# Six-stage transformer kernel: where and by which engines the last feed-forward's weights are rounded

## The chip, the cores and the metric

One core of one Trainium2 chip. The metric is device time in microseconds (us) from launch to end, median of several runs. "The profile" is one execution recorded by the hardware; its span runs from the first to the last instruction.

## What is computed

Two decoder layers on `x` of 2 x 512 tokens, width 512, each step followed by a residual add and a layer norm: causal attention with rotary embedding, cross attention with normalised queries and keys, a four-expert feed-forward; then causal attention, masked grouped cross attention, and an 8-bit feed-forward. Each attention has 16 heads of 128. Of the last step (the changed one):

```python
def _reorder_quantize_x(x, idx):
    scale = jnp.max(jnp.abs(x)) / GLOBAL_DIV
    xr = (x / scale)[:, idx]
    scale_x = jnp.max(jnp.abs(xr), axis=1, keepdims=True) / FP8_MAX
    return (_fp8(xr / scale_x), scale_x, scale)

def _qlinear(qx, scale_x, scale, W, idx, out_idx=None):
    Wr = W[:, idx]
    w_scale = jnp.max(jnp.abs(Wr), axis=1, keepdims=True) / FP8_MAX
    qw = _fp8(Wr / w_scale)
    y = qx * scale_x @ (qw * w_scale).T * scale
    ...
```

`w_gate` and `w_up` are 1408 x 512, `w_down` is 512 x 1408. Their rounding depends on no activation, so it can be done at any earlier time.

## The kernel before

**Stages.** The program runs `self0`, `cross0`, `ffn0`, `self1`, `cross1`, `ffn1` in this order. TensorE (PE) does every f32 product as three bf16 products of high and low parts; ScalarE (ACT) writes high parts, VectorE (DVE) low parts. An attention goes over 32 units (head and batch) of four query tiles. Probabilities leave as `ph` and `pl` and are turned by DMA transposes that SyncE's queue (SP) issues one after another (`transposed`). Each engine runs its own list in written order, tied to the others by semaphores.

**The end of an attention.** After unit 31 PE projects heads 0 to 7 with Wo for token tiles 0 to 3 (96 matmuls), weighs the last unit, projects heads 0 to 7 for tiles 6, 7 and then 4, 5 (96 more; tiles 4, 5 wait for `heads_out(31)` on VectorE), and then waits until all of Wo is split (`w_split` at 2H). After that come eight rounds of 24 matmuls, heads 8 to 15 of one tile, each followed by the turning of the normalised tile two before (`turn_x`). Wo for heads 8 to 15 comes head by head: `wo(h)` on SP waits for the split of head h-2 (two buffers of `raw_q`), and `split_wo(h)` on GpSimd (POOL) makes the two parts. The residual add and statistics of a tile are on VectorE (`residual`, `normalise`), the inverse deviation on GpSimd (`inv_std`), which between tiles also splits the next stage's first weights (`start_layer`).

**Rounding the last weights.** There are 26 items (`ITEMS`): 22 of 128 x 512 ("gu", gathered by GpSimd with `indirect_dma_start`, `gather`) and four of 128 x 1408 ("d", loaded by SP, `load_down`). Each goes through `quantise` (VectorE: largest value, scale, inverse), `scaled_weights` (ScalarE), `magnify` (three instructions on VectorE), `round_rows` (one subtraction on GpSimd) and `keep` (SP writes it back to HBM). Items 0 to 7 (`EARLY`) come behind the last unit of `self0`, 8 to 11 (`LATER`) behind `heads_out(31)`, 12 to 14 inside its layer norm. Items 15 to 18, the wide ones, come behind the last unit of `self1`, ahead of `heads_out(31)`; 19 to 22 behind it; 23 to 25 inside its layer norm. SP does `keep` of the early items ahead of `wo(10)`.

**Into cross1 and ffn1.** At the start of `cross1` SP writes the 26 columns of scales to HBM in pieces of 4 bytes (`kept["s"]`) and then loads the mask, spread over 128 partitions. Nothing but the first K products goes without the mask (`any`, `mb`). At the end of `cross1` the rounded weights come back through 19 DMA transposes (`turned`), four behind each `wo(h)` from `wo(10)` on, and then the scales (`sB`). In `ffn1` VectorE multiplies the gate product by its scales (`gate`), ScalarE applies Silu, GpSimd multiplies by the up scales (`times_up`), VectorE multiplies by the up product out of PSUM (`rows`), finds the row scales (`scales`) and rounds (`round_t`); `scales`, `steps` and `round_x` are the same pattern for the activations.

Of the kernel before, what the change touches and what calls it, by code (L numbers as in the profile page):

```python
# [112 lines left out]
def build(nc, a, out, kept):  # L113
    ctx = ExitStack()
    with ctx:
        def sb(name, shape, dt, where=ctx):
# [51 lines left out]
        idx_in, q_a, q_s, q_m, q_ok, s_kept, s_in, wt_in, row_y = (  # L168
            sem(x) for x in ("idx_in", "q_a", "q_s", "q_m", "q_ok", "s_kept", "s_in", "wt_in", "row_y"))
# [3 lines left out]
        fg_mm, fu_mm, g_ok, gs_ok, fs_ok, fy_ok = (sem(x) for x in ("fg_mm", "fu_mm", "g_ok", "gs_ok", "fs_ok", "fy_ok"))  # L173

        idb_ok = sem("idb_ok")
        row_in = [sem(f"row_in{i}") for i in range(4)]
# [60 lines left out]
        for li, L in enumerate(stages):  # L237
# [86 lines left out]
        def slot(k):  # L324

            return k % 4 if k < 15 else (k - 15) % 2 if k < 19 else (k - 19) % 4

        def earlier(k, kind):

            return sum(ITEMS[j][0] == kind and slot(j) == slot(k) for j in range(k))  # L330

        def item_buffers(k):

            m, w = mem[names.index("self0" if k < 15 else "self1")], FI if ITEMS[k][0] == "d" else D
            y, r = (t[:, slot(k) * w:slot(k) * w + w] for t in (m["wy"], m["wr"]))
            s = slot(k) % 2 if k < 15 else slot(k)
            return y, m["wm"][:, s * w:s * w + w], r

        def items_done(k, ring):

            return k - ring + 1 if k < 15 else (k - 1 if k >= 17 else 0) if k < 19 else max(19, k - 3)
# [7 lines left out]
        def _(sp):  # L349
# [23 lines left out]
            for li, L in enumerate(stages):  # L373
# [108 lines left out]
                for k in LATER.get(L.name, ())[:-IN_LN]:  # L482
                    keep(k)
# [6 lines left out]
        def _(pool):  # L490
# [67 lines left out]
            def gather(k):  # L558

                i = ITEMS[k][1]  # L560
                if items_done(k, 4) > 0:
                    pool.wait_ge(q_ok, items_done(k, 4))
                nc.gpsimd.indirect_dma_start(out=item_buffers(k)[0], out_offset=None, in_=a["wgate" if i < IT else "wup"],
                                             in_offset=bass.IndirectOffsetOnAxis(ap=idx[:, i % IT:i % IT + 1].bitcast(mybir.dt.uint32), axis=0)).then_inc(row_in[slot(k)], 16)

            def round_rows(k):

                y, M, q = item_buffers(k)
                pool.wait_ge(q_m, k + 1)
                if k == 19:  # L570
                    pool.wait_ge(q_kept[1], 16 * earlier(18, "gu") + 32)
                if earlier(k, "gu") + earlier(k, "d") and k not in (15, 16):
# [926 lines left out]
```

## Time and profile before

| | |
|---|---|
| median of 3 runs | 2785.51 us (2782.92 to 2787.16) |
| the profiled execution | 2783.92 us, span 2782.1 us |
| mean granted TensorE clock | 0.952 of full speed |
| PE, DVE, ACT, POOL busy | 89%, 67%, 56%, 28% of the span |
| first projection products of heads 8 to 15 | 518.2 us (`self0`), about 1312 (`cross0`), 1921.5 (`self1`), 2573.6 (`cross1`) |

Times in the trace count from the span's start. An idle time in brackets is that of the engine just before the instruction, with the instruction or transfer that ended it. L12 is line 12 of the kernel. Idle time of an engine on which nobody waits costs nothing.

### The profile page before, as it was taken

The page shows a single profiled execution, that of the slowest core. Times are in us where ns is not written, and L with a number is a line of the kernel's source. Part 1 is how long each engine was busy: PE and PEld are TensorE (multiplying, and loading weights), DVE is VectorE, ACT ScalarE, POOL GpSimd, SP SyncE. Part 2 cuts the span into 40 slices and gives each one's busy share as a digit, 9 for nine tenths or more (in the row PEclk, how much of TensorE's full clock was granted, in tenths as well). Part 3 has the DMA queues.
Part 4 walks back from the last instruction along what each step waited for, and adds up shares of the span by engine and source line. Part 5 has one row for each costly group of instructions (what it writes and reads, how often), then busy time and mean ns, then how long its engine had stood idle before and what let it go on. Part 6 is the DMA issues. An engine that isn't in the chain of part 4 may idle for free. (4 is left out here: it accounts for less than half of the span.)

```text
span 2782.1 us, 58623 instructions
## 1 busy us (share of the span) xinstructions
PE 2465.7 (89%) x21584; PEld 1580.1 (57%) x21584; DVE 1854.6 (67%) x3337; ACT 1567.3 (56%) x2692; POOL 778.9 (28%) x705
## 2 busy tenths in 40 slices
PE   6888888879999999999789999995699999997864
PEld 4555555446666666665456666652366666663322
DVE  4667776557777777772565666655488888881687
ACT  4666665148877887882244555530177777771232
POOL 4565666811110011122241222226100011022132
PEclk9999999989999999999899999997799999998886
DMA  3333335425666666665213434343287777786000
GB/s 89 84 70 82 82 71 112 118 44 107 115 117 115 109 109 114 115 126 125 101 59 65 101 79 101 80 111 94 12 149 152 146 145 147 145 164 136 10 0 31
DMA packets 777602, 273.62 MB, mean 98 GB/s; under 512 B 746096, under 2 KB 748912, under 8 KB 775792
## 3 DMA queue, kind: packets, MB, share of 16 engines
q1 hardware_dynamic: 775696, 265.85, 46.1%
q0 software_dynamic: 1760, 5.77, 0.8%
q8 instruction: 98, 1.61, 0.2%
q14 instruction: 48, 0.39, 0.0%
HBM read 84.55 MB, written 6.44 MB: 33 GB/s over the span
## 5 line engine op out<-in xcount | busy, mean ns | idle before, releaser
L860 ACT ACTIVATE ph<-p,ri 128x1024 bf16<-128x1024 f32 (+4 forms) x512 | 437.4, 854 | 473.5 <-DVE ri L1162 396.2
L1172 DVE SCALAR_TENSOR_TENSOR pl<-p,ri,ph 128x1024 bf16<-128x1024 f32 (+4 forms) x512 | 511.7, 1000 | 138.4 <-issue 74.2
L1232 PE MATMUL ps<-wo_hi,v_hi 128*128 128x128 bf16 x2688 | 479.1, 220 | 60.3 <-DMA wo_lo<-pl 59.5
L1234 PE MATMUL ps<-wo_hi,v_lo 128*128 128x128 bf16 x2688 | 478.8, 220 | 0.0
L1233 PE MATMUL ps<-wo_lo,v_hi 128*128 128x128 bf16 x2688 | 478.8, 220 | 0.0
L871 ACT ACTIVATE p<-p,nb 128x1024 f32<-128x1024 f32 (+4 forms) x512 | 435.5, 851 | 46.8 <-DVE nb L1155 36.7
L1232 PEld LDWEIGHTS ps<-wo_hi,v_hi 128*128 128x128 bf16 x2688 | 263.6, 98 | 130.2 <-DMA wo_lo<-pl 80.1
L1232 PE MATMUL ps<-k_hi,q_hi 128*128 128x512 bf16 (+3 forms) x768 | 271.9, 354 | 37.3 <-DVE k_lo L1125 31.0
L1233 PEld LDWEIGHTS ps<-wo_lo,v_hi 128*128 128x128 bf16 x2688 | 263.8, 98 | 38.9
L1234 PE MATMUL ps<-k_hi,q_lo 128*128 128x512 bf16 (+3 forms) x768 | 271.6, 354 | 0.0
L1233 PE MATMUL ps<-k_lo,q_hi 128*128 128x512 bf16 (+3 forms) x768 | 271.5, 354 | 0.0
L1234 PEld LDWEIGHTS ps<-wo_hi,v_lo 128*128 128x128 bf16 x2688 | 264.1, 98 | 0.0
L1232 PE MATMUL ps<-wo_hi,oT_hi 128*128 128x512 bf16 x512 | 199.3, 389 | 54.0 <-POOL wo_lo L517 38.3
L512 POOL TENSOR_SCALAR wkv_hi<-raw_kv 128x1024 bf16<-128x1024 f32 (+1 forms) x56 | 50.6, 903 | 649.5 <-PE ps L1234 457.3
L1232 PE MATMUL ps<-xT_hi,wq_hi 128*128 128x512 bf16 x512 | 198.2, 387 | 24.5 <-DVE k_lo L1117 14.1
L1233 PE MATMUL ps<-wo_lo,oT_hi 128*128 128x512 bf16 x512 | 198.6, 388 | 0.0
L1234 PE MATMUL ps<-wo_hi,oT_lo 128*128 128x512 bf16 x512 | 198.4, 387 | 0.0
L1233 PE MATMUL ps<-xT_lo,wq_hi 128*128 128x512 bf16 x512 | 197.9, 386 | 0.0
L1234 PE MATMUL ps<-xT_hi,wq_lo 128*128 128x512 bf16 x512 | 197.8, 386 | 0.0
L1157 DVE CUSTOM_DVE_ANT_0 p<-ps,rk,nq 128x1024 f32<-128x1024 f32 x128 | 163.2, 1275 | 51.1 <-PE ps L1234 51.0
L634 POOL TENSOR_TENSOR nq<-nq,half_neg 128x4 f32<-128x4 f32 x32 | 32.4, 1012 | 549.1 <-DVE nq L1106 549.1
L1232 PE MATMUL ps<-wkv_hi,xT_hi 128*128 128x128 bf16 x1024 | 179.8, 222 | 0.0
(187 smaller groups left out, 5875.9 us busy)
## 6 DMA issues: line engine op xcount, KB each, us to landing
raw_kv<-in_wkvself SPq DMA_DIRECT2D x32, 512.0 KB
raw_q<-in_wqself SPq DMA_DIRECT2D x32, 256.0 KB
wo_hi<-ph SPq DMA_TRANSPOSE x512, 3.2
wo_lo<-pl SPq DMA_TRANSPOSE x512, 3.1
raw_q<-in_woself SPq DMA_DIRECT2D x32, 256.0 KB
raw_q<-in_wqcross SPq DMA_DIRECT2D x32, 256.0 KB
raw_q<-in_wocross SPq DMA_DIRECT2D x32, 256.0 KB
raw_kv<-in_wkvcross SPq DMA_DIRECT2D x24, 256.0 KB
```

What stands on the lines that cost most here:

```text
L512: nc.gpsimd.tensor_scalar(hi, src, 1.0, 1.0, ALU.mult, ALU.mult).then_inc(w_hi, 1)
L634: nc.gpsimd.tensor_tensor(r, r, half_neg[:, 0:QT], ALU.pow).then_inc(q_norm, 1)
L860: nc.scalar.activation(m["ph"][:, qt % 2, 0:w], m["p"][:, qt % 2, 0:w], ACT.Copy, scale=ri[:, qt % 2:qt % 2 + 1]).then_inc(p_norm, 1)
L871: nc.scalar.activation(prob, prob, ACT.Exp, scale=1.0 if L.rms else -1.0, bias=nb[:, qt % 2:qt % 2 + 1], accum_out=rs[:, qt % 2:qt % 2 + 1 ...
L1157: ins = nc.vector.tensor_tensor_reduce(in1=m["rk"][:, n % 2, :], scale=m["nq"][:, n % 2, qt:qt + 1], op0=ALU.mult, **kw)
L1172: nc.vector.scalar_tensor_tensor(out=m["pl"][:, qt % 2, 0:w], in0=m["p"][:, qt % 2, 0:w], scalar=ri[:, qt % 2:qt % 2 + 1], in1=m["ph"][:, ...
L1232: nc.tensor.matmul(o, l(0), r(0), start=first, stop=False)
L1233: nc.tensor.matmul(o, l(0), r(1), start=False, stop=False)
L1234: return nc.tensor.matmul(o, l(1), r(0), start=False, stop=last)
```

## The change

The wide items move from `self1` to the end of `cross0` and use the memory of `ffn0`'s weights. `self0` takes items 0 to 10 (seven early, four later), `cross0` items 11 to 14, `self1` items 15 to 25 (seven early, four later); none is left inside a layer norm. GpSimd's subtraction goes: ScalarE now writes two scaled copies, and VectorE does one bit operation and two `scalar_tensor_tensor`. The second copy lies in the probabilities' buffer `m["p"]`, so ScalarE first waits for the last `pl`. Gathers have 6 buffers in `self0` and 11 in `self1`, and all are issued in a row behind the last unit. In `cross0` SP waits for the last unit's output, loads two wide items, and puts `keep` and `load_down` of the next ones between `wo(11)`, `wo(12)` and `wo(13)`. In `cross1` the mask is loaded ahead of the 4-byte writes, and `wo(10)` to `wo(15)` go ahead of the 19 transposes. GpSimd starts two pieces of the next stage's weights ahead of the first `inv_std`. In `ffn1` the up product is multiplied by its scales on VectorE (`up`), out of PSUM, and PE's up product of a tile now follows its gate product, two tiles ahead. The core of the diff:

```diff
@@ -310,10 +308,9 @@
-        ITEMS = [("gu", i) for i in range(15)] + [("d", t) for t in range(D // P)] + [("gu", i) for i in range(15, GU)]
-        EARLY = {"self0": range(0, 8), "self1": range(15, 19)}
-        LATER = {"self0": range(8, 15), "self1": range(19, 26)}
-        IN_LN = 3
+        ITEMS = [("gu", i) for i in range(IT)] + [("d", t) for t in range(D // P)] + [("gu", i) for i in range(IT, GU)]
+        EARLY = {"self0": range(0, 7), "self1": range(15, 22)}
+        LATER = {"self0": range(7, 11), "cross0": range(11, 15), "self1": range(22, 26)}
         X_COL, T_COL = GU + D // P, GU + D // P + NT
         HALF_UP = 1.5 * 2.0 ** 14
@@ -354,13 +353,13 @@
             def load_down(k):
                 t = ITEMS[k][1]
-                if items_done(k, 2) > 0:
-                    sp.wait_ge(q_ok, items_done(k, 2))
+                if t >= 2:
+                    sp.wait_ge(q_ok, k - 1)
                 sp.dma_start(item_buffers(k)[0], a["wdown"][t * P:(t + 1) * P, :]).then_inc(wd_in[t % 2], 16)
@@ -408,17 +407,14 @@
-                for k in LATER.get(names[li - 1], ())[-IN_LN:] if li else ():
-                    keep(k)
-                if L.masked:
-                    sp.wait_ge(q_a, len(ITEMS))
-                    sp.dma_start(kept["s"].rearrange("(c p) -> p c", p=P), q_scale[:, 0:X_COL], allow_slow_non_contiguous=True).then_inc(s_kept, 16)
...
                 if L.masked:
                     sp.wait_ge(ln_x, NT * li)
                     sp.dma_start(mem[li]["m8"][:, :, :], a["mask"].partition_broadcast(P)).then_inc(const_in, 16)
+                    sp.wait_ge(q_a, len(ITEMS))
+                    sp.dma_start(kept["s"].rearrange("(c p) -> p c", p=P), q_scale[:, 0:X_COL], allow_slow_non_contiguous=True).then_inc(s_kept, 16)
@@ -455,32 +451,33 @@
-                if L.name == "self1":
-                    load_down(15)
-                    load_down(16)
                 transposed(UNITS - 1, None, QT - 1)
                 wo(8)
                 wo(9)
                 for k in EARLY.get(L.name, ()):
                     keep(k)
-                    if L.name == "self1" and k + 2 < 19:
-                        load_down(k + 2)
+                if L.rms:
+                    sp.wait_ge(o_mm, c["u"] + UNITS)
+                    sp.wait_ge(p_lo, c["s"] + QT * UNITS)
+                    load_down(11)
+                    load_down(12)
+                for h in range(10, H):
+                    wo(h)
+                    if L.rms and h in (11, 12):
+                        keep(h)
+                        load_down(h + 2)
+                for k in LATER.get(L.name, ())[2 if L.rms else 0:]:
+                    keep(k)
                 if L.masked:
                     sp.wait_ge(job_mm, c["job"] + L.before(UNITS + 1))
                     for i in range(4):
-                        sp.wait_ge(q_kept[i], 16 * sum(slot(k) == i for k in range(len(ITEMS))))
+                        sp.wait_ge(q_kept[i], 16 * sum(kept_slot(k) == i for k in range(len(ITEMS))))
+                    for ch in range(2 * XC + IT):
+                        sp.dma_start_transpose(*turned(ch)).then_inc(wt_in, 16)
                     sp.wait_ge(s_kept, 16)
-                for h in range(10, H):
-                    wo(h)
-                    if L.masked:
-                        for ch in range(4 * (h - 10), min(4 * (h - 10) + 4, 2 * XC + IT)):
-                            sp.dma_start_transpose(*turned(ch)).then_inc(wt_in, 16)
-                if L.masked:
...
-                for k in LATER.get(L.name, ())[:-IN_LN]:
-                    keep(k)
@@ -558,22 +555,10 @@
-                if items_done(k, 4) > 0:
-                    pool.wait_ge(q_ok, items_done(k, 4))
+                if k in range(6, 11):
+                    pool.wait_ge(q_ok, k - 5)
...
-            def round_rows(k):
...
-                nc.gpsimd.tensor_tensor(q, y, M, ALU.subtract).then_inc(q_ok, 1)
-                if ITEMS[k][0] == "gu" and k + 4 in range(0, 15 if k < 15 else 26):
-                    gather(k + 4)
@@ -608,17 +593,8 @@
-                    def times_up(t):
-                        pool.wait_ge(fs_ok, t + 1)
-                        nc.gpsimd.tensor_tensor(m["SG"][:, t % 2, :], m["SG"][:, t % 2, :], m["sB"][:, FI:2 * FI], ALU.mult).then_inc(gs_ok, 1)
-
-                    pool.wait_ge(s_in, 16)
-                    times_up(0)
-                    for t in range(NT):
-                        if t + 1 < NT:
-                            times_up(t + 1)
-                        if t:
-                            inv_std(t - 1)
+                    for t in range(NT - 1):
+                        inv_std(t)
                     inv_std(NT - 1)
@@ -675,28 +651,22 @@
-                if L.name == "self0":
+                if L.causal:
                     pool.wait_ge(idx_in, 16)
-                    for k in range(4):
-                        gather(k)
-                for k in EARLY.get(L.name, ()):
-                    round_rows(k)
-                if L.name == "self1":
-                    for k in range(19, 23):
+                    for k in range(0, 11) if L.rope else range(15, 26):
                         gather(k)
                 pool.wait_ge(o_mm, c["u"] + UNITS)
                 for h in range(8, H):
                     split_wo(h)
-                for k in LATER.get(L.name, ())[:-IN_LN]:
-                    round_rows(k)
                 following = stages[li + 1]
                 pieces = range(0) if following is None else range(0 if following.rms else 4, 6)
+                ahead = 2
+                for piece in pieces[:ahead]:
+                    start_layer(li + 1, piece)
                 for t in range(NT):
-                    if t < len(pieces):
-                        start_layer(li + 1, pieces[t])
                     inv_std(t)
-                    if L.name in LATER and t >= NT - IN_LN:
-                        round_rows(LATER[L.name][t - NT])
+                    if t + ahead < len(pieces):
+                        start_layer(li + 1, pieces[t + ahead])
@@ -722,8 +692,11 @@
-                y, n = item_buffers(k)[0], column(k)
+                (y, M, _), n, ring = item_buffers(k), column(k), 1 if ITEMS[k][0] == "d" else 2
                 act.wait_ge(q_a, k + 1)
+                if local(k) >= ring:
+                    act.wait_ge(q_ok, k - ring + 1)
+                nc.scalar.activation(M, y, ACT.Copy, scale=q_up[:, n:n + 1])
                 nc.scalar.activation(y, y, ACT.Copy, scale=q_inv[:, n:n + 1]).then_inc(q_s, 1)
@@ -889,10 +862,12 @@
+                if L.name in EARLY:
+                    act.wait_ge(p_lo, c["s"] + QT * UNITS)
                 for k in EARLY.get(L.name, ()):
                     scaled_weights(k)
                 heads_out(UNITS - 1, None)
-                for k in LATER.get(L.name, ())[:-IN_LN]:
+                for k in LATER.get(L.name, ()):
                     scaled_weights(k)
@@ -901,8 +876,6 @@
                     for t in range(NT):
-                        if L.name in LATER and t >= NT - IN_LN:
-                            scaled_weights(LATER[L.name][t - NT])
                         x_part(li + 1, NT * (li + 1) + t, t, t)
@@ -931,24 +904,22 @@
-            def magnify(k):
-
-                y, M, _ = item_buffers(k)
+                scales(column(k), y).then_inc(q_a, 1)
+
+            def round_item(k):
+
+                y, M, q = item_buffers(k)
                 dve.wait_ge(q_s, k + 1)
-                if items_done(k, 2) > 0:
-                    dve.wait_ge(q_ok, items_done(k, 2))
-                own(nc.vector.tensor_scalar(M.bitcast(I32), y.bitcast(I32), 0x7F800000, None, ALU.bitwise_and))
-                own(nc.vector.tensor_scalar(M, M, 2.0 ** -6, 1.5 * 2.0 ** 20, ALU.max, ALU.mult))
-                nc.vector.tensor_tensor(y, y, M, ALU.add).then_inc(q_m, 1)
+                steps(M)
+                own(nc.vector.scalar_tensor_tensor(out=y, in0=M, scalar=HALF_UP, in1=y, op0=ALU.max, op1=ALU.add))
+                if local(k) >= (1 if ITEMS[k][0] == "d" else 4):
+                    dve.wait_ge(q_kept[kept_slot(k)], kept_count(k))
+                nc.vector.scalar_tensor_tensor(out=q, in0=M, scalar=HALF_UP, in1=y, op0=ALU.max, op1=ALU.subtract, reverse1=True).then_inc(q_ok, 1)
             def quantise_run(ks):
@@ -1048,13 +1019,17 @@
+                    def up(t):
+                        dve.wait_ge(fu_mm, t + 1)
+                        if t >= 2:
+                            dve.wait_ge(qt_ok, t - 1)
+                        nc.vector.tensor_tensor(m["row"][:, t % 2, :], ps[:, 3:6, :].rearrange("p a n -> p (a n)")[:, 0:FI], m["sB"][:, FI:2 * FI], ALU.mult).then_inc(u_ok, 1)
+
                     def rows(t):
                         y = m["row"][:, t % 2, :]
-                        dve.wait_ge(fu_mm, t + 1)
-                        dve.wait_ge(gs_ok, t + 1)
-                        if t >= 2:
-                            dve.wait_ge(qt_ok, t - 1)
-                        nc.vector.scalar_tensor_tensor(out=y, in0=ps[:, 3:6, :].rearrange("p a n -> p (a n)")[:, 0:FI], scalar=q_scale[:, X_COL + t:X_COL + t + 1],
+                        dve.wait_ge(fs_ok, t + 1)
+                        dve.wait_ge(u_ok, t + 1)
+                        nc.vector.scalar_tensor_tensor(out=y, in0=y, scalar=q_scale[:, X_COL + t:X_COL + t + 1],
                                                        in1=m["SG"][:, t % 2, :], op0=ALU.mult, op1=ALU.mult).then_inc(row_y, 1)
                         dve.wait_ge(row_y, t + 1)
@@ -1071,10 +1046,12 @@
+                    up(0)
                     for t in range(NT):
                         rows(t)
                         if t + 1 < NT:
                             gate(t + 1)
+                            up(t + 1)
                         round_t(t)
                         if t:
@@ -1297,7 +1271,7 @@
-                            pe.wait_ge(row_y if part else g_ok, t)
+                            pe.wait_ge(u_ok if part else g_ok, t)
                         for n, (lo, hi) in enumerate(CH):
@@ -1321,13 +1295,13 @@
+                    product(1, 1)
                     turn_qx(c["ln"], m, 6)
                     turn_qx(c["ln"], m, 7)
                     for t in range(NT):
-                        if t + 1 < NT:
-                            product(1, t + 1)
                         if t + 2 < NT:
                             product(0, t + 2)
+                            product(1, t + 2)
                         turn_rows(t)
                         pe.wait_ge(qt_T, t + 1)
                         for i in range(IT):
```

## Rows read from the trace of the kernel before

**Rows 1.** Waits, whole span: total us, times, longest.

```profile
PE ps L1232 <- POOL wo_lo L517: 38.3, 3, 18.2
PE ps L1238 <- DVE xf L1007: 30.2, 12, 5.5
```

**Rows 2.** Timeline of PE, first attention's end: start us, us, [idle before <-what ended it].

```profile
518.17 0.62 PE L1232 MATMUL ps<-wo_hi,oT_hi 128*128 128x512 bf16 x1 [6.53 <-POOL wo_lo L517]
...
581.30 0.61 PE L1232 MATMUL ps<-cT_hi,wkv_hi 128*128 128x512 bf16 x1 [1.42 <-DVE xT_lo L927]
```

**Rows 3.** Timelines of SyncE's queue and GpSimd, first attention's end.

```profile
478.66 19.92 SPq L357 DMA_DIRECT2D kept_gu<-wr  x8
...
501.55 0.34 SPq L426 DMA_DIRECT2D raw_q<-in_woself  x1
...
516.97 1.15 POOL L517 TENSOR_TENSOR wo_lo<-raw_q,wo_hi 128x512 bf16<-128x512 f32 x1
```

**Rows 4.** Groups of instructions, whole span: busy us, mean ns of one | idle before.

```profile
L979 DVE SCALAR_TENSOR_TENSOR xrow<-xM,xrow 128x512 f32<-128x512 f32 x8 | 5.5, 693 | 0.3
L965 DVE TENSOR_REDUCE q_max<-row 128x1 f32<-128x1408 f32 x8 | 13.0, 1620 | 0.3
L972 DVE TENSOR_SCALAR M<-M 128x1408 int32<-128x1408 int32 x8 | 7.2, 894 | 12.3 <-ACT row L779 12.3
L1066 DVE SCALAR_TENSOR_TENSOR row<-M,row 128x1408 f32<-128x1408 f32 x8 | 13.0, 1625 | 0.3
L778 ACT ACTIVATE M<-row,q_up 128x1408 f32<-128x1408 f32 x8 | 11.7, 1468 | 22.7 <-DVE q_up L968 22.7
```

**Rows 5.** Timelines of GpSimd and VectorE, second attention's end.

```profile
1307.89 1.16 POOL L517 TENSOR_TENSOR wo_lo<-raw_q,wo_hi 128x512 bf16<-128x512 f32 x1
...
1317.41 0.69 DVE L999 TENSOR_TENSOR xf<-ps,xf 128x512 f32<-128x512 f32 x1 [24.58 <-PE ps L1234]
...
1355.86 0.69 DVE L999 TENSOR_TENSOR xf<-ps,xf 128x512 f32<-128x512 f32 x1 [2.93 <-PE ps L1234]
...
1360.61 0.69 DVE L927 TENSOR_TENSOR xT_lo<-ps,xT_hi 128x512 bf16<-128x512 f32 x1 [0.18 <-ACT xT_hi L707]
```

**Rows 6.** Windows of 72 matmuls: length; PE, PEld, DVE, ACT, POOL busy; clock; DMA.

```profile
1312.20:1327.74 15.54, 15.54 (x74) 7.17 (x73) 3.59 (x7) 0.00 (x0) 1.80 (x4) 1.00 0.13 52
1921.51:1939.90 18.39, 18.38 (x72) 8.51 (x72) 3.85 (x7) 0.00 (x0) 12.93 (x14) 0.85 0.37 115
```

**Rows 7.** Loads of down-projection rows, issue to landing; their write-backs on SyncE's queue.

```profile
DMA to landing us min/median/max: 4.2/4.4/6.2
...
1865.08 0.34 SPq L357 DMA_DIRECT2D kept_d<-wr  x1
...
1878.36 0.34 SPq L357 DMA_DIRECT2D kept_d<-wr  x1
```

**Rows 8.** Timeline of PE, from the third attention's end into the fourth.

```profile
1895.38 0.62 PE L1232 MATMUL ps<-wo_hi,oT_hi 128*128 128x512 bf16 x1 [15.76 <-DVE oT_lo L1136]
...
1921.51 0.62 PE L1232 MATMUL ps<-wo_hi,oT_hi 128*128 128x512 bf16 x1 [13.51 <-POOL wo_lo L517]
...
1983.27 0.61 PE L1232 MATMUL ps<-cT_hi,wkv_hi 128*128 128x512 bf16 x1 [1.42 <-DVE xT_lo L927]
...
2002.61 0.61 PE L1232 MATMUL ps<-xT_hi,wq_hi 128*128 128x512 bf16 x1 [14.06 <-DVE k_lo L1117]
```

**Rows 9.** DMA issues from 1980 to 2003 us: KB each, us to landing.

```profile
m<-in_mask SPq DMA_DIRECT2D x1, 256.0 KB, 17.5
kept_s<-q_scale SPq DMA_DIRECT2D x1, 13.0 KB, 15.6
```

**Rows 10.** Timeline of PE, fourth attention's end.

```profile
2573.59 0.61 PE L1232 MATMUL ps<-wo_hi,oT_hi 128*128 128x512 bf16 x1 [18.23 <-POOL wo_lo L517]
```

**Rows 11.** Window of one last feed-forward tile; rounding instruction, ns min/median/max.

```profile
2702.73:2719.27 16.54, 11.33 (x46) 5.09 (x46) 14.89 (x15) 5.04 (x5) 5.16 (x4) 0.71 0.00 1
...
L1070 DVE SCALAR_TENSOR_TENSOR Q<-M,row x8: 1625/4454/4467, 2648.8 to 2761.7; 128x1408 bf16<-128x1408 f32 x8
```

More of the change, by code:

```diff
@@ L166, in build @@
         gu_mm, silu_ok, prod_ok, inter_hi, inter_lo = (sem(x) for x in ("gu_mm", "silu_ok", "prod_ok", "inter_hi", "inter_lo"))
-        idx_in, q_a, q_s, q_m, q_ok, s_kept, s_in, wt_in, row_y = (
-            sem(x) for x in ("idx_in", "q_a", "q_s", "q_m", "q_ok", "s_kept", "s_in", "wt_in", "row_y"))
+        idx_in, q_a, q_s, q_ok, s_kept, s_in, wt_in, row_y = (
+            sem(x) for x in ("idx_in", "q_a", "q_s", "q_ok", "s_kept", "s_in", "wt_in", "row_y"))
         wd_in, q_kept = [sem("wd_in0"), sem("wd_in1")], [sem(f"q_kept{i}") for i in range(4)]
@@ L172, in build @@
         t_amax, t_scaled, t_sum, qt_ok, qt_mm, qt_T = (sem(x) for x in ("t_amax", "t_scaled", "t_sum", "qt_ok", "qt_mm", "qt_T"))
-        fg_mm, fu_mm, g_ok, gs_ok, fs_ok, fy_ok = (sem(x) for x in ("fg_mm", "fu_mm", "g_ok", "gs_ok", "fs_ok", "fy_ok"))
+        fg_mm, fu_mm, g_ok, u_ok, fs_ok, fy_ok = (sem(x) for x in ("fg_mm", "fu_mm", "g_ok", "u_ok", "fs_ok", "fy_ok"))
         idb_ok = sem("idb_ok")
-        row_in = [sem(f"row_in{i}") for i in range(4)]
+        row_in = [sem(f"row_in{i}") for i in range(11)]
         by_name = {L.name: L for L in LAYERS}
@@ L322, in column, with local, kept_slot, kept_count @@
             return ITEMS[k][1] + (GU if ITEMS[k][0] == "d" else 0)
[L324 to L330, printed above, removed]
+        def local(k):
+            return k if k < 11 else k - 11 if k < 15 else k - 15
         def item_buffers(k):
[L334 to L341, printed above, removed]
+            j = local(k)
+            if ITEMS[k][0] == "d":
+                hi, lo = (t[:, :, :, :].rearrange("p e c n -> p (e c n)") for t in mem[names.index("ffn0")]["gu"])
+                return hi.bitcast(F32)[:, j % 2 * FI:j % 2 * FI + FI], lo.bitcast(F32)[:, 0:FI], hi[:, 4 * FI:5 * FI]
+            m, s = mem[names.index("self0" if k < 11 else "self1")], j % (6 if k < 11 else 11)
+            return m["wy"][:, s * D:s * D + D], m["p"][:, j % 2, :], m["wr"][:, j % 4 * D:j % 4 * D + D]
+        def kept_slot(k):
+            return 0 if ITEMS[k][0] == "d" else local(k) % 4
+        def kept_count(k):
+            return 16 * sum(kept_slot(j) == kept_slot(k) for j in range(k))
         CH = [(0, 512), (512, 1024), (1024, FI)]
@@ L560, in gather @@
                 i = ITEMS[k][1]
-                if items_done(k, 4) > 0:
-                    pool.wait_ge(q_ok, items_done(k, 4))
+                if k in range(6, 11):
+                    pool.wait_ge(q_ok, k - 5)
                 nc.gpsimd.indirect_dma_start(out=item_buffers(k)[0], out_offset=None, in_=a["wgate" if i < IT else "wup"],
-                                             in_offset=bass.IndirectOffsetOnAxis(ap=idx[:, i % IT:i % IT + 1].bitcast(mybir.dt.uint32), axis=0)).then_inc(row_in[slot(k)], 16)
-            def round_rows(k):
[L568 to L572, printed above, removed]
-                    pool.wait_ge(q_kept[slot(k)], 16 * (earlier(k, "gu") + earlier(k, "d")))
-                nc.gpsimd.tensor_tensor(q, y, M, ALU.subtract).then_inc(q_ok, 1)
-                if ITEMS[k][0] == "gu" and k + 4 in range(0, 15 if k < 15 else 26):
-                    gather(k + 4)
+                                             in_offset=bass.IndirectOffsetOnAxis(ap=idx[:, i % IT:i % IT + 1].bitcast(mybir.dt.uint32), axis=0)).then_inc(row_in[local(k)], 16)
             for li, L in enumerate(stages):
@@ L676, in _ @@
                 units(pool, unit, L)
-                if L.name == "self0":
+                if L.causal:
                     pool.wait_ge(idx_in, 16)
-                    for k in range(4):
-                        gather(k)
-                for k in EARLY.get(L.name, ()):
-                    round_rows(k)
-                if L.name == "self1":
-                    for k in range(19, 23):
+                    for k in range(0, 11) if L.rope else range(15, 26):
                         gather(k)
@@ L932, in quantise @@
             def quantise(k):
[L934 removed]
+                (kind, i), y = ITEMS[k], item_buffers(k)[0]
                 if kind == "gu":
[L936 removed]
+                    dve.wait_ge(row_in[local(k)], 16 * (1 if k < 11 or local(k) >= 11 else 2))
                 else:
                     dve.wait_ge(wd_in[i % 2], 16 * (i // 2 + 1))
[L939 to L951 removed]
+                scales(column(k), y).then_inc(q_a, 1)
+            def round_item(k):
+                y, M, q = item_buffers(k)
+                dve.wait_ge(q_s, k + 1)
+                steps(M)
[3 more added lines that the diff above has]
+                nc.vector.scalar_tensor_tensor(out=q, in0=M, scalar=HALF_UP, in1=y, op0=ALU.max, op1=ALU.subtract, reverse1=True).then_inc(q_ok, 1)
             def quantise_run(ks):
@@ L959, in quantise_run @@
                         quantise(k + 1)
-                    magnify(k)
+                    round_item(k)
             def scales(n, src):
@@ L1207, in _ @@
                 heads_out(UNITS - 1, None)
-                later = LATER.get(L.name, ())
-                quantise_run(later[:-IN_LN])
+                quantise_run(LATER.get(L.name, ()))
                 last_attention = names[li + 1] == "ffn1"
@@ L1221, in _ @@
                         round_x(mem[li + 1], k - 2)
-                    if L.name in LATER and NT - IN_LN <= k < NT:
-                        quantise_run(later[k - NT:k - NT + 1] if k < NT - 1 else later[-1:])
                     if 0 <= k - 3 < NT and not last_attention:
```

10 lines of the change are left out of this document (2 added, 8 removed).

## The prediction

> **What bounds the kernel now.** I read the waits first, over the whole span. TensorE (PE) is the busiest engine, so time is won only where PE stands. Two sums catch the eye [rows 1]: 38.3 us in three waits for GpSimd's split of Wo, and 30.2 us for normalised tiles, which VectorE hands over late where items lie inside the norm. PE's timeline places the three: 6.53 us at 518.17 [rows 2], 13.51 at 1921.51 [rows 8], 18.23 at 2573.59 [rows 10]. It shows two more: 15.76 us for the last head output at 1895.38, and 14.06 us at 2002.61 inside the first products of `cross1` [rows 8]. `cross0` has no such stall: its last Wo split ends at 1307.89 + 1.16 = 1309.05 [rows 5]; the first tile's residual starts at 1317.41, so with 24 matmuls in 15.54 / 3 = 5.18 us [rows 6] PE needed Wo at about 1312.2, a margin of 3.2 us. Last, one tile of `ffn1` takes 16.54 us, of which VectorE is busy 14.89 and PE 11.33 [rows 11]: VectorE sets that pace. Its rounding instruction takes 4.45 us as median and 1.63 us in the one tile in which GpSimd has no product [rows 11].
>
> A stall also costs what follows it. 72 projection matmuls took 15.54 us at granted clock 1.00 and 18.39 us at 0.85 behind the 13.51 us stall [rows 6]: 2.9 us of ramp.
>
> **Price of one item.** VectorE now does, for 512 columns, a largest value (0.69, as [rows 4]'s first row), three scalars (0.2 each, an estimate: 0.15 us and the gap), one bit operation (half of 0.89 [rows 4]) and two combinations of 0.69: 3.1 us. Before, eight items left SyncE (SP) in 19.92 us, 2.8 us apart [rows 3]. So GpSimd's work moves over at almost no change of pace. For 1408 columns: 1.62 + 0.6 = 2.2 us to the scale, 2 x 1.47 = 2.9 us on ScalarE, 0.89 + 2 x 1.63 + gaps = 4.2 us of rounding [rows 4].
>
> **self0.** The first item is written at 478.66 [rows 3]; the seventh is ready 6 x 3.1 later, less one look-ahead of 1.3: about 496. `wo(10)`, queued behind seven `keep`, goes then instead of at 501.55. From that issue to the last split took 516.97 + 1.15 - 501.55 = 16.6 us [rows 3]; now it ends at 512.6. PE needs it at 518.17 - 6.53 = 511.6 [rows 2]: 1 us of stall is left. GpSimd's eleven gathers (some 1 us each) end before the last unit is weighed. `heads_out(31)`, behind seven items on VectorE, comes at about 497; PE asks two rounds before 511.6, at 501.2. From there: eight rounds of 5.18, six turnings of 0.44 (an estimate from the spacing of 5.62 between residuals), and the end as in `cross0`, where no item lies in the norm: 1360.61 + 0.69 - 1355.86 = 5.4 us [rows 5]. With 0.5 us for the context pieces ahead of the first `inv_std`, the first K product of `cross0` comes at 512.6 + 41.4 + 2.7 + 0.5 + 5.4 = 562.6, against 581.30 [rows 2]: **gain 19** (15 to 21). The wait for the last `pl` costs nothing: VectorE makes it before its first item.
>
> **cross0.** This is the bill. SP waits for the last unit, at 1312.2 less 96 matmuls (20.7): 1291.5. Loads 11 and 12 go out, 4.4 us to landing [rows 7]; then scale 2.2, ScalarE 2.9, rounding 4.2, signals and GpSimd's share 0.8: item 11 is ready at 1306. Only then do `keep(11)`, load 13 and `wo(12)` pass. Load 13: 4.4 + 2.2 + 4.2 + 0.7 = 11.5, `keep(12)` at 1317.5 to 1318. Load 14 then goes ahead of `wo(13)`: 4.4 us, and three heads at 16.6 / 6 = 2.8: 12. Last split about 1330. Needed at 1312.2: stall 17.5, ramp 2.9: **loss 20**. The nearest rows for a round trip are the old write-backs of wide items, 1878.36 - 1865.08 = 13.3 us apart [rows 7] with one more GpSimd step; two of 13.3 in place of 14.5 + 11.5 give the same sum. Bounds: trips of 8 us, loss 8; trips of 18 us, loss 34. Items 13 and 14 end near 1339, beside the first rounds; `keep(14)` delays `ffn0`'s first loads to 1340; they are first used when the norm is over, at 1361 + 20: nothing.
>
> First the row on contention: 4.45 against 1.63 us [rows 11]. The Trainium skill (SBUF — State Buffer, "Who interferes with whom") says that a VectorE instruction with two SBUF inputs waits for a GpSimd instruction that reads SBUF, and the reverse, by an exclusive lock; the trace agrees. By that rule each rounding step that meets a split loses the whole split, and the new roundings, with more such instructions than the old, lie beside GpSimd's Wo splits. In this kernel that is 1.16 us for a low part [rows 5]; two a trip in `cross0` would make the loss 25 instead of 20. What it would do to all three attentions is a rival below.
>
> **self1.** The wide items and their loads go, seven narrow ones come. PE needs `heads_out` at 1895.38 - 15.76 = 1879.6 [rows 8]; before that lie 48 + 96 matmuls of 0.216 us, so the last unit's softmax ends about 1850, and the items can start. Seven take 22 us: `heads_out` at 1872 to 1874. `wo(10)` at 1872, last split at 1889; needed 48 matmuls (10.4) after 1879.6, at 1890.0. The eleven gathers go out without a wait and end before the split of head 8. Both stalls go. First K product at 1890.0 + 41.4 + 2.7 + 5.4 + 0.5 = 1940, against 1983.27 [rows 8]: **gain 43** (38 to 45). What is late next is Wo, with 1 us to spare.
>
> **The mask.** It took 17.5 us from issue to landing, behind 13 KB of scales that took 15.6 [rows 9]. The K products run 2002.61 - 14.06 - 1983.27 = 5.3 us; a mask loaded first should land some 4 us after issue (720 KB took 4.4 [rows 7]), the search for its largest value takes over 2, so 1 to 1.5 us stay: **gain 12.5**. Lower bound 0, if the spread over 128 partitions is slow by itself; upper 14. The scales' 15.6 us move behind the mask, and their end is about where the first probability transposes begin; nothing else on SP waits.
>
> **cross1.** `wo(10)` is issued right behind the first split, and without four transposes between heads the chain takes what it did in `cross0`: about 16 us from its issue. PE needs Wo at 2573.59 - 18.23 = 2555.4 [rows 10]; the splits start 96 matmuls earlier, at 2534.7, the first is done 1.9 us later, and the last at 2553. The 19 transposes and the scales move behind it: at 1.5 us each, 29 us from 2548, done by 2580; the eight rounds last until 2555.4 + 41.4 + 1 = 2598, and only then does `ffn1` ask for them. **Gain 21**: the stall and the ramp (18 to 22).
>
> **ffn1.** VectorE's tile loses 4.45 - 1.63 = 2.8 and a 1.3 us wait for ScalarE that the new product fills, and gains one product of 1.62: 16.54 - 2.5 = 14.0. Six such tiles give 15.2 us; the start wins about 1.8, less than GpSimd's first product, since PE's second up product now precedes two turnings. PE has 11.33 us of work at clock 0.71 and fits in 14.0, unless half clock returns. **Gain 16** (8 to 20).
>
> **Sum.** 19 - 20 + 43 + 12.5 + 21 + 16 = 91.5 us. On the profiled execution (2783.92, of which the span is 2782.1) that gives 2692.4; the median lies 1.6 us higher, so the forecast is **2694 us**. A measurement of this kernel can tell about 0.2%, 5.6 us, from no change.
>
> **Rivals.**
> - **The lock costs more** (chance 0.12). If items take 4.2 instead of 3.1 us, `wo(10)` is 7 us later: a stall of 8 and its ramp in `self0`, 6 and its ramp in `self1`, 8 more in `cross0`: 28 us less, 2722. For it: 4.45 us in [rows 11]; against: VectorE's pace was 2.8 with GpSimd's subtraction in every item. The rule of the Trainium skill (SBUF — State Buffer) named above speaks for this case.
> - **The mask is slow by itself** (0.1): 2694 + 12.5 = 2706. For it: no row shows it alone. Against: it landed right behind the scales, on one queue.
> - **cross0 hides more** (0.1): if the two loads land together and trips are 8 us, the loss is 8: 2682.
> - **Slower than before** (0.03): SP's queue in `cross0`. Every microsecond in the two round trips goes to PE through `wo(12)` to `wo(15)`. It decides when the two trips take 26 + 91.5 = 118 us, 59 each; at 65 each the kernel ends at 2797. The old trips of 13.3 us [rows 7] speak against it.
> - **No effect** (0.01): the stalls would have to have another cause than the releasers named.
>
> The forecast's own case has 0.64. The range is 2674 to 2724: up to the lock's case, and down to 2682 less the upper ends of `ffn1` and `self1`. Faster 0.96, same 0.01, slower 0.03.
>
> **What would show it.** In the new profile: waits for Wo near 1 us in `self0` and none in `self1` and `cross1`; one of 15 to 20 us in `cross0`, with `wo(12)` and `wo(13)` issued behind two write-backs; no wait for `oT_lo` in `self1`; the mask landed within 5 us; `Q` at 1.6 us and tiles of 14 us in `ffn1`. I am wrong if `cross0`'s stall is under 8 or over 34 us, if a wait for Wo above 5 us is left elsewhere, or if `ffn1`'s tiles take over 15.5 us because PE, not VectorE, sets the pace.

## The result and the profile after

The changed kernel takes **2699.99 us** (median of 4 runs, 2695.85 to 2703.11), the kernel before 2784.72 (4 runs): a ratio of 0.9694, 95% interval 0.9677 to 0.9711. The forecast was 2694, its range 2674 to 2724. The profiled execution took 2701.27 us, with a span of 2699.4 us against 2782.1: 82.7 us less.

The forecast rested on where PE stands, so the waits come first, over the whole span (total us, times, longest). This is the profile of the changed kernel:

```profile
PE ps L1206 <- POOL wo_lo L514: 29.0, 3, 20.0
...
PE ps L1212 <- DVE xf L978: 11.9, 8, 4.6
```

The three waits for the split of Wo still exist, 29.0 us in place of 38.3 [rows 1], but not in the same places. PE's timeline shows them (start us, us, and in brackets the idle time before and what ended it), with the first K products and the first query product:

```profile
516.46 0.62 PE L1206 MATMUL ps<-wo_hi,oT_hi 128*128 128x512 bf16 x1 [4.47 <-POOL wo_lo L514]
...
568.74 0.61 PE L1206 MATMUL ps<-cT_hi,wkv_hi 128*128 128x512 bf16 x1 [1.42 <-DVE xT_lo L900]
...
1319.04 0.61 PE L1206 MATMUL ps<-wo_hi,oT_hi 128*128 128x512 bf16 x1 [19.98 <-POOL wo_lo L514]
...
1902.58 0.62 PE L1206 MATMUL ps<-wo_hi,oT_hi 128*128 128x512 bf16 x1 [4.52 <-POOL wo_lo L514]
...
1954.70 0.61 PE L1206 MATMUL ps<-cT_hi,wkv_hi 128*128 128x512 bf16 x1 [1.42 <-DVE xT_lo L900]
...
1960.62 0.39 PE L1206 MATMUL ps<-xT_hi,wq_hi 128*128 128x512 bf16 x1 [1.28 <-DVE k_lo L1094]
```

Set beside [rows 2, 8, 10], `self0` and `self1` keep a stall of 4.5 us each, `cross0` has a new one of 19.98, and `cross1` has none. The 15.76 us wait for `oT_lo` is gone, and the 14.06 us before the first query product has become 1.28. Behind each stall 72 matmuls take about 18.1 us, as they did in the second window of [rows 6] (window; PE, PEld, DVE, ACT, POOL busy; clock; DMA):

```profile
516.46:534.65 18.19, 18.19 (x74) 8.77 (x75) 3.58 (x7) 0.00 (x0) 13.50 (x12) 0.86 0.50 149
1319.04:1337.20 18.16, 18.16 (x76) 8.01 (x77) 7.89 (x11) 1.15 (x1) 1.80 (x4) 0.87 0.52 194
1902.58:1920.62 18.04, 18.04 (x74) 8.72 (x75) 3.58 (x7) 0.00 (x0) 7.08 (x10) 0.87 0.13 48
```

**Where a rounding meets a split.** The timelines of VectorE, GpSimd and SP's queue at the end of `self0`:

```profile
489.06 0.69 DVE L919 SCALAR_TENSOR_TENSOR wy<-p,wy 128x512 f32<-128x512 f32 x1
...
491.57 1.08 DVE L943 TENSOR_SCALAR p<-p 128x512 int32<-128x512 int32 x1
492.68 1.53 DVE L919 SCALAR_TENSOR_TENSOR wy<-p,wy 128x512 f32<-128x512 f32 x1
494.24 0.98 DVE L922 SCALAR_TENSOR_TENSOR wr<-p,wy 128x512 bf16<-128x512 f32 x1
495.15 1.38 DVE L943 TENSOR_SCALAR p<-p 128x512 int32<-128x512 int32 x1
...
492.45 1.22 POOL L514 TENSOR_TENSOR wo_lo<-raw_q,wo_hi 128x512 bf16<-128x512 f32 x1
493.63 1.06 POOL L509 TENSOR_SCALAR wo_hi<-raw_q 128x512 bf16<-128x512 f32 x1
494.77 1.47 POOL L514 TENSOR_TENSOR wo_lo<-raw_q,wo_hi 128x512 bf16<-128x512 f32 x1
...
498.38 12.77 SPq L422 DMA_DIRECT2D raw_q<-in_woself  x6
...
514.94 1.46 POOL L514 TENSOR_TENSOR wo_lo<-raw_q,wo_hi 128x512 bf16<-128x512 f32 x1
```

Each of an item's two rounding instructions takes 0.69 us where GpSimd is idle; beside the splits of heads 8 and 9 those of the sixth item take 1.53 and 0.98, and the bit operation, 0.42 elsewhere, takes 1.08 and 1.38 in the sixth and seventh. That is 2.75 us more for the two items, and `wo(10)` is issued at 498.38. The chain behind it takes 516.40 - 498.38 = 18.0 us.

**`cross0`**, SP's queue and the last splits:

```profile
1278.37 0.81 SPq L363 DMA_DIRECT2D gu_hi<-in_wdown  x2
...
1292.82 0.34 SPq L356 DMA_DIRECT2D kept_d<-gu_hi  x1
1293.21 0.43 SPq L363 DMA_DIRECT2D gu_hi<-in_wdown  x1
1293.68 0.46 SPq L422 DMA_DIRECT2D raw_q<-in_wocross  x1
1304.48 0.34 SPq L356 DMA_DIRECT2D kept_d<-gu_hi  x1
...
1305.34 7.09 SPq L422 DMA_DIRECT2D raw_q<-in_wocross  x3
...
1313.39 2.40 POOL L514 TENSOR_TENSOR wo_lo<-raw_q,wo_hi 128x512 bf16<-128x512 f32 x1
1315.76 1.99 POOL L509 TENSOR_SCALAR wo_hi<-raw_q 128x512 bf16<-128x512 f32 x1
1317.83 1.16 POOL L514 TENSOR_TENSOR wo_lo<-raw_q,wo_hi 128x512 bf16<-128x512 f32 x1
```

The two round trips take 14.4 us (1278.37 to 1292.82) and 11.7 us (to 1304.48), and `wo(12)` and `wo(13)` stand behind them. Then three instructions of the last splits take 1.26, 2.40 and 1.99 us instead of 0.62, 1.16 and 0.62, beside item 13 on VectorE.

**The mask and `ffn1`.** DMA issues from 1945 to 1975 (KB, us to landing), the window of one tile, and the last rounding step (ns min/median/max):

```profile
m<-in_mask SPq DMA_DIRECT2D x1, 256.0 KB, 4.7
kept_s<-q_scale SPq DMA_DIRECT2D x1, 13.0 KB, 14.1
```

```profile
2625.40:2639.20 13.80, 9.79 (x46) 4.29 (x46) 13.49 (x16) 5.60 (x5) 2.30 (x2) 0.88 0.00 0
...
L1045 DVE SCALAR_TENSOR_TENSOR Q<-M,row x8: 1624/1624/1625, 2584.9 to 2678.2; 128x1408 bf16<-128x1408 f32 x8
```

The mask lands in 4.7 us in place of 17.5 [rows 9]. A tile takes 13.80 us in place of 16.54 [rows 11]: VectorE is busy 13.49 of them, so it still sets the pace, and `Q` never takes more than 1.63 us.

The spans between fixed points of PE's timeline give the account: `self0` +12.6, `cross0` -22.3, `ffn0` with `self1` +38.3, the mask +13.4, the rest of `cross1` +22.6, `ffn1` +18.2, in all 82.8 us.

### The profile page after: what moved, and what is told of

Its sections match the earlier page's. It is cut to its first block and busy times, and to the rows that moved or that the text cites. A ratio compares the mean times of both kernels' runs of the same rounds, so it can differ in the third digit from the quotient of the medians.

```text
span 2699.4 us, 58652 instructions
## 1 busy us (share of the span) xinstructions
PE 2454.4 (91%) x21584; PEld 1576.5 (58%) x21584; DVE 1853.7 (69%) x3371; ACT 1586.2 (59%) x2718; POOL 721.8 (27%) x671
```

## The experiments

All ten kernels are edits of the changed kernel (2700.0 us); times are medians of 4 runs (5 for the last one), ratios are to the kernel before. The kernel before ran again beside each of them, the changed kernel did not; the medians of the former were 2783.9 to 2785.9, so a difference to 2700.0 us can be off by some 2 us.

### Three parts undone, one at a time

**The scales ahead of the mask again** (u_mask):

```diff
-sp.dma_start(mem[li]["m8"]..., a["mask"]...)
 sp.wait_ge(q_a, len(ITEMS))
 sp.dma_start(kept["s"]..., q_scale..., ...)
+sp.dma_start(mem[li]["m8"]..., a["mask"]...)
```

> The changed kernel with one part undone: in cross1 the 13 KB of scales (4-byte pieces) are written again ahead of the mask. Theory: the mask was late only because it stood behind them on the same queue, so the first masked score waits again 17 to 19 us after the first K product (5.92 us in the changed kernel) and the time is 13.4 us above it, about 2713 us. Rival (the mask's spread over 128 partitions is slow by itself, and something else brought the gain): the wait and the time stay within 2 us of the changed kernel's.

2714.8 us, ratio 0.9753 (0.9736 to 0.9769): 14.8 us above the changed kernel. DMA and PE of this run:

```profile
m<-in_mask SPq DMA_DIRECT2D x1, 256.0 KB, 18.8
...
1970.73 0.61 PE L1206 MATMUL ps<-xT_hi,wq_hi 128*128 128x512 bf16 x1 [16.58 <-DVE k_lo L1094]
```

The mask takes 18.8 us again, and PE stands for 16.58. The spread over 128 partitions is not slow by itself: 4.7 us where nothing is ahead of it.

**The transposes between the loads of Wo again** (u_cross1):

```diff
 for h in range(10, H):
     wo(h)
+    if L.masked:
+        for ch in range(4 * (h - 10), min(4 * (h - 10) + 4, 2 * XC + IT)):
+            sp.dma_start_transpose(*turned(ch)).then_inc(wt_in, 16)
```

> The changed kernel with one part undone: cross1's 19 weight transposes stand again between and behind the loads of Wo for heads 10 to 15. Theory: each load waits for four transposes ahead of it, so the last split of Wo is some 18 us late, and the ramp behind the stall comes back: 21 to 23 us above the changed kernel, about 2722 us, with a wait of 17 to 19 us on wo_lo of cross1. Rival (the chain of Wo was freed by VectorE's items, which have gone from cross1's neighbourhood, not by the order on SP): no stall, less than 3 us.

2721.6 us, ratio 0.9772 (0.9756 to 0.9788): 21.6 us above. SP's queue, the second half, and PE:

```profile
2519.39 2.43 SPq L473 DMA_TRANSPOSE cT_hi<-kept_d  x2
2521.86 2.58 SPq L473 DMA_TRANSPOSE cT_lo<-kept_d  x2
2524.48 0.58 SPq L422 DMA_DIRECT2D raw_q<-in_wocross  x1
2525.10 3.73 SPq L473 DMA_TRANSPOSE wkv_hi<-kept_d  x3
2528.88 0.58 SPq L422 DMA_DIRECT2D raw_q<-in_wocross  x1
...
2533.87 0.61 PE L1208 MATMUL ps<-wo_hi,oT_hi 128*128 128x512 bf16 x1 [17.90 <-POOL wo_lo L516]
```

Four transposes take 5 to 8 us of the queue ahead of a load, the three ahead of the last one 3.7, and the stall of 17.90 us is back. In the changed kernel the six loads go out within 11.9 us, and the transposes behind them are done before `ffn1` asks.

**GpSimd multiplies by the up scales again** (u_up):

```diff
+def times_up(t):   # GpSimd
+    pool.wait_ge(fs_ok, t + 1)
+    nc.gpsimd.tensor_tensor(m["SG"]..., m["SG"]..., m["sB"][:, FI:2 * FI], ALU.mult).then_inc(u_ok, 1)
-nc.vector.tensor_tensor(m["row"]..., ps..., m["sB"][:, FI:2 * FI], ALU.mult).then_inc(u_ok, 1)
```

> The changed kernel with one part undone: in ffn1 GpSimd multiplies the gate row by the up scales again, and PE's products stand in the order of before. Theory: Q (the last rounding step) takes 4.4 us again instead of 1.63 and a tile 16.5 us instead of 13.75, so 16 to 18 us above the changed kernel, about 2717 us. Rival (the other parts of the change made ffn1 faster too, for instance through the clock): less than 12 us.

PE's up products also stand in the order of before in this kernel. 2717.1 us, ratio 0.9758 (0.9742 to 0.9774): 17.1 us above. `Q` is back at 4.45 us as median. The undone parts cost 14.8, 21.6 and 17.1 us, against 13.4, 22.6 and 18.2 in the account of the traces: the gains are independent and lie where the account puts them.

### Why Q took 4.45 us: three kernels with an unneeded GpSimd instruction

**Beside the rounding** (x_beside). The instruction adds work, takes none away, and nothing waits for it; it is called where `times_up` was:

```diff
+def beside(t):
+    pool.wait_ge(fs_ok, t + 1)
+    own(nc.gpsimd.tensor_tensor(raw_kv...[:, 0:FI], m["sB"][:, 0:FI], m["sB"][:, FI:2 * FI], ALU.mult))
```

> The changed kernel as it is in its work and order, and beside it in ffn1 one GpSimd product of 1408 columns a tile, from two SBUF operands into a buffer that nothing reads, issued on the same signal as the product of before. No engine waits for its result. Theory of the lock (two-input VectorE instructions and GpSimd's exclude each other): Q goes back to about 4.4 us in the tiles that it meets, and a tile to about 16.5 us: 14 to 18 us above the changed kernel, near 2716 us. Rival (the old tile was long because of the chain of waits through GpSimd, and Q's 4.45 us held a wait): Q stays at 1.6 us and the time within 2 us of the changed kernel.

2720.4 us (2711.9 to 2720.8), ratio 0.9758 (0.9740 to 0.9777): 20.4 us above. VectorE and GpSimd in one tile:

```profile
2646.99 1.62 DVE L1050 SCALAR_TENSOR_TENSOR row<-M,row 128x1408 f32<-128x1408 f32 x1
...
2648.65 4.46 DVE L1054 SCALAR_TENSOR_TENSOR Q<-M,row 128x1408 bf16<-128x1408 f32 x1
...
2647.38 4.25 POOL L598 TENSOR_TENSOR raw_kv<-sB 128x1408 f32<-128x1408 f32 x1 [6.11 <-ACT SG L753]
```

No data passes between the two, and still `Q` takes 4.46 us. The instruction that was there first, the first rounding step, keeps its 1.62; GpSimd's product starts 1.23 us before that ends and grows by about as much (4.25 against 3.19 by itself, below). `Q`, issued while the product runs, grows by 2.83. The two take turns.

A shared bandwidth could stretch both too. What speaks against it is already in the changed kernel, where GpSimd handles one column per tile:

```profile
2613.57 1.68 DVE L1032 SCALAR_TENSOR_TENSOR row<-row,q_scale,SG 128x1408 f32<-128x1408 f32 x1
...
2613.81 1.85 POOL L571 TENSOR_TENSOR rstd<-rstd,half_neg 128x1 f32<-128x1 f32 x1
...
2682.74 0.57 POOL L571 TENSOR_TENSOR rstd<-rstd,half_neg 128x1 f32<-128x1 f32 x1
```

One column needs hardly any bandwidth. Begun 0.24 us behind VectorE's two-operand product it takes 1.85 us and ends 0.41 us after it; by itself it takes 0.57. It stands until VectorE is done.

**One operand** (x_one): `tensor_scalar(raw_kv..., m["sB"][:, 0:FI], 2.0, ...)` in its place.

> x_beside with one change: GpSimd's unneeded instruction has one SBUF operand (a product with a constant, 1408 columns) instead of two. Theory, by the Trainium skill (SBUF — State Buffer, 'Who interferes with whom'), under which any GpSimd instruction that reads SBUF holds the port: Q is still stretched, by GpSimd's own duration, to 3 us or more in the tiles that it meets, and the time is 6 us or more above the changed kernel. Rival (only the two-operand form shuts VectorE out): Q at 1.62 us and no more than 3 us above the changed kernel.

2717.1 us, ratio 0.9756 (0.9740 to 0.9773): 17.1 us above. `Q` takes 4.42 us as median, so one SBUF operand on GpSimd is enough.

**Five us earlier** (x_psum): the two-operand product again, on another signal (and issued for tile t, not t + 1, ahead of the inverse deviation of tile t - 1).

```diff
-pool.wait_ge(fs_ok, t + 1)
+pool.wait_ge(t_amax, t + 1)
```

> x_beside with one change: the same two-operand GpSimd product of 1408 columns is issued 5 us earlier in the tile, on the signal that the largest value is known, so that it runs beside VectorE's two products that read PSUM and one SBUF operand (1.62 us each) and the bit operation with one operand (0.89), some 4.1 us in all. In x_beside the two engines took turns: GpSimd's product started beside the first rounding step (1.63 us, not stretched) and Q stood until it was done. Theory: only VectorE instructions with two SBUF operands are shut out; GpSimd's product takes about 3 us there, Q 1.62, and the time stays within 4 us of the changed kernel, below 2704. Rival (any VectorE instruction that reads SBUF is shut out, or the two slow each other by bandwidth): the products beside it take 3 to 4.4 us, and the time is about 2716 as in x_beside.

2700.4 us, ratio 0.9696 (0.9680 to 0.9713): the changed kernel's time. The same two engines:

```profile
2641.56 1.62 DVE L1027 TENSOR_TENSOR SG<-ps,sB 128x1408 f32<-128x1408 f32 x1
2643.10 1.61 DVE L1033 TENSOR_TENSOR row<-ps,sB 128x1408 f32<-128x1408 f32 x1
2644.63 1.02 DVE L950 TENSOR_SCALAR M<-M 128x1408 int32<-128x1408 int32 x1
...
2647.35 1.62 DVE L1052 SCALAR_TENSOR_TENSOR Q<-M,row 128x1408 bf16<-128x1408 f32 x1
...
2641.72 3.19 POOL L598 TENSOR_TENSOR raw_kv<-sB 128x1408 f32<-128x1408 f32 x1 [1.88 <-DVE q_up L946]
```

The same product costs 20 us of the kernel beside roundings and nothing beside VectorE's products from PSUM. Only the bit operation shows a trace of it, 1.02 us instead of 0.89, where they overlap by 0.28 us.

### What stands in the attentions' ends, and a faster version

**Two items fewer ahead of Wo** (f_wo), in `self0` and `self1`:

```diff
-for k in EARLY.get(L.name, ()):
+for k in early[:-2]:
     keep(k)
+wo(10); wo(11)
+for k in early[-2:]:
+    keep(k)
```

> The changed kernel with one move on SP: in self0 and self1 the loads of Wo for heads 10 and 11 stand ahead of the last two early write-backs. Theory: the stall of 4.5 us on the last Wo split in both attentions comes from the wait of wo(10) for the seventh item (VectorE's), so two items less (2 x 3 us) take the stalls and the ramps of 2.5 us behind them away: 10 to 14 us below the changed kernel, about 2688 us. Rival (the PSUM banks and the splits' own pace of 2.8 us a head set the end, not the issue of wo(10)): the stalls shrink by less than 2 us and the time by less than 4.

2687.6 us, ratio 0.9653 (0.9638 to 0.9667): 12.4 us below the changed kernel. Of PE's waits for `wo_lo` one of 0.5 us and that of `cross0` are left. The wait of `wo(10)` for the seventh item made both stalls. The splits beside items are stretched here too (1.47 us for a low part), without a stall in `self0`.

**Wo ahead of the round trips in `cross0`** (f_c0a):

```diff
 wo(h)
-if L.rms and h in (11, 12):
-    keep(h)
-    load_down(h + 2)
+if L.rms and h == 14:
+    keep(11)
...
+load_down(13); keep(12); load_down(14); keep(13); keep(14)
```

> The changed kernel with SP's order changed in cross0 alone: loads of wide items 11 and 12, then Wo for heads 10 to 14 without a write-back between, then the write-backs and the loads of items 13 and 14. Theory: the stall of 19.98 us in cross0 stands in the two round trips that wo(12) and wo(13) wait for; it goes, with 2.5 us of ramp, but items 13 and 14 now come between VectorE and the first residuals, which costs some 10 to 14 us in the norm: net 8 to 12 us below the changed kernel, about 2690 us. Rival (the stall is set by contention on the DMA queue or by stretched splits, not by the wait): a stall of 12 us or more stays on wo_lo.

2691.9 us, ratio 0.9664 (0.9650 to 0.9679): 8.1 us below.

```profile
1302.25 0.39 PE L1211 MATMUL ps<-wo_hi,oT_hi 128*128 128x512 bf16 x1 [2.78 <-POOL wo_lo L519]
...
1330.41 0.48 PE L1217 MATMUL ps<-ident,xf 128*128 128x128 f32 x1 [10.76 <-DVE xf L983]
```

Of the stall of 19.98 us 2.78 are left, so SP's order made it. But items 13 and 14, loaded later now, still come ahead of the first residual on VectorE, and PE stands 10.76 us for a normalised tile.

**Those two items inside the norm** (f_c0b); ScalarE's part of them moves between its pieces of tiles 0 and 2 in the same way:

```diff
-quantise_run(LATER.get(L.name, ()))
+quantise_run(LATER.get(L.name, ())[:2 if L.rms else 4])
...
+if L.rms and k in (1, 3):
+    quantise(13 + k // 2)
+if L.rms and k in (2, 4):
+    round_item(12 + k // 2)
```

> The kernel of f_c0a, and items 13 and 14 rounded inside cross0's layer norm, between VectorE's tiles, instead of ahead of it. Theory: neither Wo nor the first residual waits then, 18 to 22 us below the changed kernel, about 2680 us. Rival (VectorE is full in the norm, so that 2 x 8 us of items delay the last tiles by as much): 6 to 10 us below it only, with PE waiting for xf or xT of the last tiles.

2680.0 us, ratio 0.9621 (0.9607 to 0.9636): 20.0 us below. The tile's wait is gone; a stall for Wo of 4.34 us stands. The splits of GpSimd ahead of it:

```profile
1289.88 1.92 POOL L514 TENSOR_SCALAR wo_hi<-raw_q 128x512 bf16<-128x512 f32 x1 [0.96 <-DMA raw_q<-in_wocross]
1291.88 2.41 POOL L519 TENSOR_TENSOR wo_lo<-raw_q,wo_hi 128x512 bf16<-128x512 f32 x1
1294.26 0.61 POOL L514 TENSOR_SCALAR wo_hi<-raw_q 128x512 bf16<-128x512 f32 x1
...
1297.53 1.73 POOL L514 TENSOR_SCALAR wo_hi<-raw_q 128x512 bf16<-128x512 f32 x1 [1.41 <-DMA raw_q<-in_wocross]
1299.34 2.40 POOL L519 TENSOR_TENSOR wo_lo<-raw_q,wo_hi 128x512 bf16<-128x512 f32 x1
```

Four of them lie beside the roundings of items 11 and 12 and take 8.46 us in place of 3.54 (0.61 or 1.16 each): 4.9 us, about the stall. That this is its whole cause was not tried.

**Both** (f_best):

> f_wo and f_c0b together. The stalls lie in different stages, so the gains should add: 28 to 36 us below the changed kernel, about 2668 us, 4% below the kernel before. Rival (what self0 gains is given back in cross0, because the write-backs come later there): their sum less 8 us or more.

**2669.2 us** (2668.2 to 2671.7), ratio 0.9585 (0.9571 to 0.9598): 30.8 us below the changed kernel. The single gains were 12.4 and 20.0, so they add but for 1.6 us, within the spread of the runs.

## Why the prediction was right

The forecast's sum was 91.5 us, the measured one 82.8, and each of the six terms has the sign and the place that were forecast. Two of the signs named beforehand did not come: a wait for Wo near 1 us in `self0` and none in `self1`. Both waits are 4.5 us, just under the 5 us that would have counted against the forecast. `self0` lies below its own bounds (15 to 21) and `cross1` a little above (18 to 22). And the sum is nearer than its terms: `self0`, `cross0` and `self1` came out 13.4 us worse together, the other three 4.7 us better. That they offset each other is luck.

- **`self0`**: 19 expected, 12.6 measured, the worst term relative to its size. The step that failed is "the seventh is ready 6 x 3.1 later ... about 496": it was 2.4 us later. The items' pace of 2.95 us instead of 3.1 won 0.9, the stretch shown above cost 2.75, and the rest is a shorter look-ahead and SP's issue of the seventh write-back. The chain then took 18.0 instead of 16.6: its twelve split instructions took 13.3 us together against 11.1 in the kernel before, beside VectorE's later items (read from the traces, not tried by itself). With that Wo missed PE by 4.47 us instead of 1. A ramp of 18.19 - 15.54 = 2.65 us, left out for so short a stall, came on top: 2.4 + 1.4 + 2.65 = 6.4.
- **`cross0`**: 20 expected, 22.3 measured. The trips were priced at 14.5 and 11.5 and took 14.4 and 11.7. The last leg took 14.5 us instead of 12. Its own terms, 4.4 and three times 2.8, add to 12.8; the rest fits the three split instructions that met item 13's rounding (3.3 us). f_c0a shows that SP's order is the cause. The bounds were added wrongly: by the forecast's own method trips of 8 and 18 us give losses of 10 and 30, not 8 and 34. Nothing hung on them.
- **`self1`**: 43 expected, 38.3 measured. Counted in the time of the kernel before (9.7 us less, by the start of `ffn0`) `wo(10)` went out at 1874.8 instead of 1872: the first item began at 1851.5 instead of 1850, and the seven took 23.3 us instead of 22. The last split ended at 1892.8 instead of 1889, 18.0 us after that issue, and PE asked for it at 1888.4 instead of 1890.0. "1 us to spare" became a stall of 4.52 and its ramp. The wait for `oT_lo` went as forecast.
- **The mask**: 12.5 expected, 13.4 measured. **`cross1`**: 21 and 22.6. **`ffn1`**: 16 and 18.2, tiles of 13.80 us instead of 14.0, and a start that won 1.8. The forecast's terms, 15.2 and 1.8, add to 17.0, not 16.
- **The rival of the lock** was true in its mechanism and too dear in its price. It supposed that every item takes 4.2 us; items take 2.95 us (two bit operations in a row begin at 485.66 and 488.61), and of the seven early ones in `self0` only the two beside the splits of heads 8 and 9 are stretched (in `self1` only the sixth, by 1.6 us). The rule of the Trainium skill (SBUF — State Buffer, "Who interferes with whom"), by which a VectorE instruction with two SBUF inputs and a GpSimd instruction that reads SBUF exclude each other, agrees with `Q` in all three runs above. The same section says that a VectorE instruction with at most one SBUF input does not contend outside its two-port modes, and that these modes do: the products from PSUM at 1.62 us agree with the first. The bit operations at 1.08, 1.38 and 1.02 us would agree with the second if they run in such a mode; no run here shows the mode, only their pace.
- **"The mask is slow by itself"** fell with u_mask, **"`cross0` hides more"** and "Slower than before" with the trips of 14.4 and 11.7 us, and "No effect" with the ratio.

## What to carry to other kernels

Where a queue issues loads and write-backs in order, a write-back that waits for a compute result holds back every load behind it: put what TensorE needs next ahead of it (worth 20 us here, together with the two items that had to move for it). Place work of GpSimd by what VectorE does beside it: the same product of 3.2 us cost 20 us beside two-operand instructions in SBUF, and nothing beside products from PSUM. And when a stall is forecast to shrink to 1 us, price its end with the stretch and the ramp still in: here 3.8 us of delay in the chain ahead of it, less what there was to spare, went to TensorE in both attentions.

## What the runs showed that was not expected

- The bit operation on 32-bit integers takes part in the exclusion. It has one SBUF operand and handles 1408 columns in 0.89 us, where the other instructions take 1.62; beside Wo's splits it grew from 0.42 to 1.08 and 1.38 us.
- A stall of 4.5 us is followed by as slow a stretch as one of 20 us: 72 matmuls took 18.19 and 18.04 us behind 4.47 and 4.52, and 18.16 behind 19.98, at granted clocks of 0.86 to 0.87. That is a mean of the two levels: behind the stall that ends at 516.46 the granted clock was 0.50 (1.2 GHz) up to 521.50 and 1.00 (2.4 GHz) from there on. The first matmul behind each of the three stalls takes 0.61 to 0.62 us; behind 2.78 us in f_c0a, and behind 1.28 before the first query product, it takes 0.39. The idle time just before does not decide alone: the first K product, at the end of a layer norm in which PE had stood several times, takes 0.61 behind 1.42 us.
- 13 KB of scales in pieces of 4 bytes took 14.1 us to land, and the 256 KB of the mask 4.7: the small transfer is the one to issue last.
